# A graph layer on one core: query work spread over 32 steps and a 0/1 selection built on ScalarE

## The reference

```python
xn = _layernorm(x)
# graph attention over the edges
xw = (xn @ W).reshape(N, H, C)
e = leaky_relu(a_src[src] + a_dst[dst], 0.2)
ex = exp(e - m[dst])
msg = xw[src] * (ex / denom[dst])[:, :, None]
out = segment_sum(msg, dst, num_segments=N)
# linear attention over the nodes, a second-order form in q
qn, kn = _normalize(q) * ..., _normalize(k) * ...
y = A*einsum('bhni,bhnj,bhije->bhne', qn, qn, kv_mod) + B*einsum(qn, kv) + C*vsum
y = y[..., 1:] / y[..., :1];  mix = y @ Wproj.T + bproj
x = x + relu(out + bias) + mix
x = x + ffn(_layernorm(x))     # 16 experts, the best 2 of each node
```

## Time and profile before

| | |
|---|---|
| median of 3 runs | 3619.04 us (3616.8 to 3632.86) |
| the profiled execution | 3621.04 us, its span 3619.1 us |
| first to last gather of the edge stage | 592 to 2746 us |
| PE busy over the span | 2612.6 us (72%) |
| DVE busy | 2372.9 us (66%) |
| POOL busy | 2244.8 us (62%) |
| ACT busy | 1235.3 us (34%) |

### The profile page before, as it was taken

The page is one execution under the profiler, slowest core; times in us unless marked ns, Lnnn a source line. Parts: engine busy times, 40 slices in busy tenths (PEclk is TensorE's granted clock), DMA queues, the critical chain, the costliest instruction groups (busy, mean ns, idle before and its releaser), DMA issues. The chain is left out here.

```text
span 3619.1 us, 51717 instructions
## 1 busy us (share of the span) xinstructions
PE 2612.6 (72%) x12151; PEld 1706.3 (47%) x12151; DVE 2372.9 (66%) x5084; ACT 1235.3 (34%) x2615; POOL 2244.8 (62%) x2160
## 2 busy tenths in 40 slices
PE   4888874999999899998666656566663609999930
PEld 2444432444445444444444444344442607888820
DVE  5899986777777777777666667666668831111148
ACT  2333322555555555554333333333331101222210
POOL 2777764777777777767777777777776660000046
PEclk9999996999999999999888788878886559999965
DMA  4111113444444444444444444444442137777734
GB/s 126 30 31 31 31 23 94 131 124 129 128 130 123 133 128 126 126 120 129 132 130 130 133 134 134 132 132 128 134 132 54 70 118 237 227 235 236 227 121 137
DMA packets 296179, 453.38 MB, mean 125 GB/s; under 512 B 117244, under 2 KB 194073, under 8 KB 295938
## 3 DMA queue, kind: packets, MB, share of 16 engines
q0 software_dynamic: 91088, 256.16, 25.5%
q1 hardware_dynamic: 181346, 128.67, 12.5%
q10 hardware_dynamic: 23520, 66.07, 5.2%
HBM read 395.62 MB, written 56.70 MB: 125 GB/s over the span
## 5 line engine op out<-in xcount | busy, mean ns | idle before, releaser
L932 POOL DMA_INDIRECT rows_g<-node_rows,idx x1568 | 1611.1, 1027 | 576.4 <-issue 472.9
L1166 PE MATMUL p_m<-msg,sel 128*128 128x264 f32 x3520 | 1065.8, 454 | 280.5 <-DVE msg L1137 246.9
L1166 PEld LDWEIGHTS p_m<-msg,sel 128*128 128x128 f32 x3520 | 741.7, 222 | 429.8 <-issue 298.4
L1137 DVE TENSOR_TENSOR msg<-rows_g,msg 128x1024 f32<-128x1024 f32 x440 | 537.2, 1221 | 112.2 <-ACT msg L1037 92.4
L1037 ACT ACTIVATE msg<-lg 128x32 f32<-128x32 f32 x440 | 100.0, 227 | 901.9 <-DVE lg L1131 775.4
L986 ACT ACTIVATE apart<-dst_all,iota_neg 128x512 bf16<-128x512 bf16 x443 | 313.3, 707 | 60.2 <-DMA dst_all<-dst_bc 60.1
L989 ACT ACTIVATE sel_t<-apart,ones 128x512 bf16<-128x512 bf16 x443 | 319.8, 722 | 31.2 <-issue 1.0
L1752 POOL DMA_DIRECT2D slot_y<-ysb x64 | 34.6, 541 | 462.8 <-DVE ysb L1742 462.8
L1060 DVE TENSOR_TENSOR sel<-iota_bf,dst_t 128x512 f32<-128x512 bf16 x441 | 304.7, 691 | 25.3 <-issue 5.8
L1127 DVE TENSOR_TENSOR lg<-rows_g,ends 128x32 f32<-128x32 f32 x440 | 84.8, 193 | 359.7 <-SPq L953 257.2
L1002 ACT ACTIVATE qfeat<-p_scr 128x512 f32<-128x512 f32 x442 | 241.1, 596 | 212.5 <-PE p_scr L1183 176.5
(11 more groups left out here) (301 smaller groups left out, 3345.6 us busy)
## 6 DMA issues: line engine op xcount, KB each, us to landing
dst_all<-dst_bc ACTq DMA_DIRECT2D x112, 512.0 KB
wa<-in_L_ffn_w_dram SPq DMA_DIRECT2D x64, 512.0 KB, 4.0
wb<-in_L_ffn_w_dram SPq DMA_DIRECT2D x64, 512.0 KB, 5.2
rows_g<-node_rows,idx POOLq DMA_INDIRECT x1568
xs<-slot_x SPq DMA_DIRECT2D x64, 256.0 KB, 3.1
slot_y<-ysb POOLq DMA_DIRECT2D x64, 256.0 KB, 4.3
bb<-in_L_ffn_b_dram SPq DMA_DIRECT2D x64, 128.0 KB, 5.0
qs<-qn_dram ACTq DMA_DIRECT2D x14, 512.0 KB, 3.9
```

The source lines that it names most:

```text
L932: pool.indirect_dma_start(rows_g[:, j, u, :], None, node_rows, bass.IndirectOffsetOnAxis(ap=idx[q][:, j, u:u + 1], axis=0)).then_inc(gathe ...
L1137: dve.tensor_tensor(m4, g3[:, :, 0:D].rearrange("p u (h e) -> p u h e", h=H), msg[j % 2][:, :, D:ROW].unsqueeze(3).broadcast_to([P, TC, H, ...
L1166: mm = pe.matmul(p_m[j % 2][:, 0:ROW], sel[j][:, u, :], msg[j % 2][:, u, :], start=(u == 0), stop=(u == TC - 1))
```

## The change

`SPAN` goes from 16 to 32 steps, so the 13 groups fill steps 0 to 415, and the tables of `query(n, k)` are written anew on PE, ACT and DVE: at most four P tiles in a step, never in two steps on end (k = 2, 4, 9, 11, 15, 17, 21, 23), each weighed one or two steps later; reciprocals at k = 8 and 11; T at 0 and 1; projections at 30 and 31 and their additions at 0 and 1 of the next group. `FR` is 6. `sel` is no longer made by DVE: ACT makes it two steps ahead with four Squares of 128 columns (each with a column of `dst_t` as its bias), a drain and one Relu of 512 columns. `dst_t` is float32 for that. `sel_t` and `sel` each have one `apart` buffer where `sel_t` had two.

```diff
-SPAN = 2 * OCT
+SPAN = 4 * OCT
-FR = 8
+FR = 6
-        dst_t = sb("dst_t", [P, SP_, TILES_PER_CHUNK], BF16, ctx=early)
+        dst_t = sb("dst_t", [P, SP_, TILES_PER_CHUNK], ctx=early)
...
@@ ACT
+                def select(s, j):
+
+                    for u in range(TC):
+                        act.activation(apart[1][:, u * P:(u + 1) * P], iota_bf[:], ACT.Square, bias=dst_t[:, s, u:u + 1], scale=-1.0)
+                    act.drain()
+                    wait(act, msg_summed, s - R + 1)
+                    act.activation(sel[j][:].rearrange("p u n -> p (u n)"), apart[1][:], ACT.Relu, bias=ones[:, 0:1], scale=-1.0).then_inc(sel_ready, 1)
...
+                    elif k in (2, 4, 9, 11):
+                        square_pairs(n, 0, (2, 4, 9, 11).index(k))
+                    elif k in (15, 17, 21, 23):
+                        square_pairs(n, 1, (15, 17, 21, 23).index(k))
...
                     select_turned(s + 3, (k + 3) // R % 2, (j + 3) % R)
+                    select(s + 2, (j + 2) % R)
...
                 for j in range(3):
                     select_turned(j, 0, j)
+                    if j < 2:
+                        select(j, j)
@@ DVE
-                def select(s, j):
-
-                    wait(dve, msg_summed, s - R + 1)
-                    d = dst_t[:, bass.ds(s, 1), :].rearrange("p s u -> p (s u)")
-                    dve.tensor_tensor(sel[j][:], iota_bf[:].unsqueeze(1).broadcast_to([P, TC, P]),
-                                      d.unsqueeze(2).broadcast_to([P, TC, P]), ALU.is_equal).then_inc(sel_ready, 1)
...
+                    if k in (4, 6):
+                        times_gram(n, (4, 6).index(k))
+                    elif k in (8, 11):
+                        invert_norm(n, (8, 11).index(k))
+                    elif k in (15, 28):
+                        scale_y(n, (15, 28).index(k))
...
-                    j1 = (j + 1) % R
-                    select(s + 1, j1)
```

More of the change, by code:

```diff
@@ L985, in select_turned @@
                         act.wait_ge(dst_in[q], (s - q * R) * (16 // R // 2) + 16)
-                    act.activation(apart[j % 2][:], dst_all[q][:, j, :], ACT.Square, bias=iota_neg[:])
+                    act.activation(apart[0][:], dst_all[q][:, j, :], ACT.Square, bias=iota_neg[:])
                     act.drain()
                     wait(act, dst_spread, s - R + 1)
-                    act.activation(sel_t[j][:], apart[j % 2][:], ACT.Relu, bias=ones[:, 0:1], scale=-1.0).then_inc(sel_t_ready, 1)
+                    act.activation(sel_t[j][:], apart[0][:], ACT.Relu, bias=ones[:, 0:1], scale=-1.0).then_inc(sel_t_ready, 1)
+                def select(s, j):
[4 more added lines that the diff above has]
+                    act.activation(sel[j][:].rearrange("p u n -> p (u n)"), apart[1][:], ACT.Relu, bias=ones[:, 0:1], scale=-1.0).then_inc(sel_ready, 1)
                 def take_queries(n, g):
@@ L1008, in query @@
                 def query(n, k):
[L1009 to L1031, removed]
+                    if k in (0, 1):
+                        take_queries(n, k)
+                        if k == 1:
+                            load(n + 1)
+                    elif k in (2, 4, 9, 11):
+                        square_pairs(n, 0, (2, 4, 9, 11).index(k))
+                    elif k in (15, 17, 21, 23):
+                        square_pairs(n, 1, (15, 17, 21, 23).index(k))
+                    elif k in (7, 10):
+                        take_norm(n, (7, 10).index(k))
+                    elif k in (13, 25):
+                        square(n, f"S{(13, 25).index(k)}")
                 def body(s, k, n, last):
@@ L1092, in query @@
                 def query(k, n, last):
[L1093 to L1096, removed]
+                    if last is not None and (k == 0 or k == 1 and last < GROUPS_Q - 1):
+                        add_mix(last, k)
                     if n is None:
                         return
[L1099 to L1110, removed]
+                    if k in (4, 6):
[4 more added lines that the diff above has]
+                        scale_y(n, (15, 28).index(k))
                 def body(s, k, n, last):
@@ L1137, in body @@
                     dve.tensor_tensor(m4, g3[:, :, 0:D].rearrange("p u (h e) -> p u h e", h=H), msg[j % 2][:, :, D:ROW].unsqueeze(3).broadcast_to([P, TC, H, C]), ALU.mult).then_inc(msg_ready, 1)
-                select(0, 0)
                 rounds(dve, body)
@@ L1222, in query @@
                 def query(n, k):
[L1223 to L1265, removed]
@@ new lines, in query @@
+                    pairs = {2: (0, 0), 4: (0, 1), 9: (0, 2), 11: (0, 3), 15: (1, 0), 17: (1, 1), 21: (1, 2), 23: (1, 3)}
+                    sums = {3: (0, 0), 6: (0, 1), 10: (0, 2), 12: (0, 3), 16: (1, 0), 18: (1, 1), 22: (1, 2), 24: (1, 3)}
+                    if k in (0, 1):
+                        turn_queries(n, k)
+                    elif k in pairs:
+                        sum_pairs(n, *pairs[k])
+                    if k in sums:
+                        weigh(n, *sums[k])
+                    if k in (3, 5):
+                        gram(n, (3, 5).index(k))
+                    elif k in (7, 10):
+                        norm(n, (7, 10).index(k))
+                    elif k in (13, 25):
+                        sum_far(n, (13, 25).index(k))
+                    elif k in (14, 27):
+                        weigh_rest(n, (14, 27).index(k))
+                    elif k in (30, 31):
+                        project(n, k - 30)
```

## The result

The changed kernel takes 3645.18 us (median of 9 runs, 3639.5 to 3646.73), the kernel before 3618.7 us beside it (9 runs, 3610.1 to 3632.86). The ratio is 1.0066, 95% interval 1.0049 to 1.0084: slower by 0.7%, a small difference but clear of the noise. The profiled execution has a span of 3643.4 us, 24.3 us more than before.

What follows compares the result with a forecast made beforehand. POOL's gathers, one behind the other, were taken to bound the edge stage. From the profiled 3621 us, +93 of stretch and -56 of waits gave 3658, less 2 for the median: 3656 us, range 3570 to 3715.

Steps and rivals of the forecast that it cites:

- The chain: Edge stage, 592 to 2746 us: 1568 gathers one behind the other; POOL's waits for messages fall from 61 us to 5.
- ACT's loop: ACT's step with sel added, exponential to exponential: 3.49, say 3.5 us, setting the pace of steps that wait for nothing.
- the other pattern: Products about 3.6 us apart: one gather starts just ahead and goes free, the next product's is caught; 0 and 0.9 in turn.
- The stretch: Time gathers take beyond the undisturbed 0.947 us, when caught by DVE's message products: 219 us in all, against 126 before.
- that wait for no chunk: Message products without any wait, 3.5 us apart: 100 of them at 1.00 us of stretch, 100 us; 70 to 150 possible.
- delayed by four squares: Message products in steps where ACT makes four query squares, about 5.8 us apart: 91 at 0.45 us, 41 us of stretch.
- behind a reciprocal: Message products after DVE's 3.35 us reciprocal, at k = 8 and 11, 6.2 us apart: 26 with no stretch.
- that wait over 0.4 us for their chunk: The other message products, paced by the landing of their chunk, about 5.35 us apart: 223 at 0.35 us, 78 us.
- The rule for one product: A gather starting f us into a 1.22 us message product is stretched by 1.08 - f, by nothing beyond 1.08.
- rival B: Gathers in the edge stage: stretch stays at 126 us and only POOL's waits go, 3563 us; chance 0.2.
- C: Gathers in the edge stage: caught and free in turn, or random phases, 3610 to 3640 us, no change; chance 0.24.
- D: Edge stage: ACT or PE becomes the bound, at 5.3 us a step 166 us more, 3820; chance 0.06.

Runs made afterwards that it cites:

- weights_in_psum: Changed kernel with the message product's weights read from PSUM, written there by a second exponential, and two p_scr banks instead of three; 3536.88 us.
- three_more_squares_2: Changed kernel with three idle Squares of 42 columns into a spare tile after the four of sel in each step, run again; 3685.84 us.
- sel_alone: Kernel before (16 steps a group) with sel made by ACT as in the changed kernel, and six feature buffers; 3960.33 us.
- two_banks: Changed kernel with two p_scr banks instead of three and nothing else; 4247.46 us beside 4271.01 for the kernel before.

## Why the prediction was right

**The chain.** Predicted: gathers set the stage, and POOL's waits go, 61 us to 5. They went to 0. The idle time before gathers fell from 576.4 to 510.1 us, by 66 us, so the term was 10 us too small (61 read, of which I kept 5). The chain ends 26 us later than before, 2772 against 2746, and the span is longer by 24 us: the stage accounts for all of it.

**ACT's loop.** 3.49 us was worked out, 3.46 is the spacing in the step above, and the four Squares take 386 ns where 385 was interpolated. Over all 440 products of after, 79 follow the one before by 3.2 to 3.6 us, with a mean spacing of 3.49 and a mean stretch of 0.79. I had 100 at 1.00. What I had not seen is that 37 more come at about 3.0 us (3.16 was worked out for DVE's own loop); 25 of them are the steps right behind a reciprocal, whose exponential was done while DVE was still at it. They pay 0.52 each. The 17 products at 3.6 to 3.7 us pay nothing, which is the other pattern that the prediction had from 3.6 on.

**The stretch.** Predicted 219 us, measured 218. That is closer than its parts deserve, and that it meets to 1 us is luck. The 440 products of after, sorted as the prediction sorted them:

| products | predicted | measured |
|---|---|---|
| that wait for no chunk | 100 at 1.00 = 100 us | 150 at 0.57 = 86 us |
| delayed by four squares | 91 at 0.45 = 41 us | 91 at 0.38 = 35 us |
| behind a reciprocal | 26 at 0 | 26 at 0.84 = 22 us |
| that wait over 0.4 us for their chunk | 223 at 0.35 = 78 us | 173 at 0.41 = 71 us |

The rest, 4 us, lies in other instructions of DVE. The term that failed is the reciprocals': they were put at nothing because their products were to be 6.2 us apart. They are 7.1 to 7.3 us apart in 21 of 26 cases, since the reciprocal waits for ACT's norm (0.89 us in the place shown above), which the 3.16 + 3.35 us of the prediction left out. At 7.26 us its own list of starts (7.33) puts a gather at the head of the product, and the rows have it 0.09 us in. The other three terms came out 14, 6 and 7 us smaller, and so the sum hides the miss of 22. The rule for one product (stretch = 1.08 - f) held in every place shown here but for the product after the reciprocal, which is 1.16 us long and pays 0.05 less; its spacing version gave 1.00, 0.02 and 0.40 for three kernels and the rows have 0.97, 0.02 and 0.39.

**The sum.** 3656 was predicted and 3645 measured; the 10 us of the waits are the difference. The upper end of the range, 3715, does not follow from its working: 3656 + 50 is 3706, and 50 more steps at 1.00 in place of 0.35 are 33 us and not 50. Nothing hangs on it. The SBUF — State Buffer page of the Trainium skill says, under Who interferes with whom, that a DVE instruction with two SBUF inputs contends with GpSimd instructions that read SBUF; weights_in_psum agrees for the two inputs, with 218 to 1 us. The remark of the same section that a `tensor_tensor` was not seen to hold up GpSimd's DMAs does not hold for these indirect gathers (up to 2.02 us in after instead of 0.947), and rival B, which went by it, fell.

**The other rivals.** C (an even mix) would have needed a loop near 3.6 us. D (ACT as the bound) did not happen in the changed kernel, but POOL's waits in three_more_squares_2 (80 us) and sel_alone (350 us) show how close it lies. What the profile was to show: waits near 0, a mean over 1.08 us (1.086) and a clock between 0.82 and 0.96 (0.87) came. ACT's busy time was forecast at 2230 us and is 2046, since overlapping activations count once; DVE's fell by 273 and not 305 us, for the same reason.

## What to carry to other kernels

Where one engine issues transfers back to back and sets the pace, ask of every long instruction on its neighbour whether it holds that engine up, and at which offset: shortening a step can then cost more than it saves, and a padded step can be faster, as 0.29 us of idle work a step saved 79 us here. Better than tuning the offset is to remove the contention, here by reading one operand from PSUM; after that, look at what comes next, which was only 108 us away. Split a change into its halves before judging it: one half was worth 64 us alone, the other cost 90 on top of it, and 341 without it.

## What the runs showed of the hardware

- A GpSimd indirect gather that starts from 0.05 to 1.05 us into a DVE product of two SBUF inputs (1.22 us) ends 0.81 to 0.84 us after the product, wherever in it it starts (345 cases in after). One that starts before the product or in its first 0.04 us is untouched; behind a reciprocal, where the profile shows no pause before the product, the limit lies some 0.1 us earlier. With one of the inputs in PSUM nothing is stretched (mean 948 ns against a median of 946).
- The same holds within one kernel for two additions of 128x512: 20 gathers start inside `resid<-resid,b_proj` of after, and those 0.05 to 0.15 us in take 1.36 to 1.46 us; 6 start inside `resid<-resid,p_scr`, with one input in PSUM, and take 0.94 to 0.95 us.
- A comparison of 128x512 with two SBUF inputs does the same (1.42 us for a gather that starts 0.08 us into 0.68 us); four comparisons of 128 columns with a column as their scalar do not.
- On one chip the same kernel took 4271 us instead of 3619, with PE idle for up to 11 us at a time for no reason that the profile shows (two_banks). Whether it is the chip or something that went on at the time is not shown.
